# The block order of TensorE, and who rounds the staged expert rows

## The chip, the cores and the metric

One core of a Trainium2 chip runs the whole kernel in one launch. The time is the device time of an execution in microseconds (us). Before the change the median of three runs is 1381.29 us (1379.74 to 1384.87).

## The reference

The input x is 32 sequences of 128 rows and 512 columns, with a context of the same shape. Two gated residual steps follow each other:

```python
x = x + tanh(g_xattn) * attention(layernorm(x), ctx, Wq, bq, Wk, bk, Wv, bv)   # 8 heads of 16, over 512 positions
x = x + tanh(g_ffn) * ffn(layernorm(x), ...)
# attention: q, k, v = projections + bias; softmax(q k / sqrt(16)) v, in each head
# ffn: h = rmsnorm(x) * rms_weight; probs = softmax(h @ router_w); top 2 of 8 experts, weights normalised
#      moe = sum of w_e * (silu(h @ w_gate_e) * (h @ w_up_e)) @ w_down_e, plus one shared expert of the same form
```

In the attention the 128 rows of a sequence are the channels and the 512 columns are the positions. All is float32.

## The kernel before

The kernel is written engine by engine: each engine has its own list of instructions, and semaphores order them across engines. Within an engine the written order is the order of work.

The first stage is a pipeline over the 32 sequences. `TURNS` runs i from -3 to 31. In turn i TensorE works on the scores and values of sequence i, on the row maxima of sequence i + 1, on projections of sequences i + 2 and i + 3, and on the token transposes and router logits of sequence i - 3. A turn has 32 slots s, which TensorE takes in eight blocks of four (`GROUP`). In one block before the change:

1. `exp_scores` (L847) for s and s + 1: two score products in two row halves of the array, each into a bank of its own. With `take_bank` (L788) the three banks of `turning` go round among score products and side products, and a product waits until the last reader of its bank is done. For scores that is ScalarE's exponential (L1342).
2. `max_scores` (L823) twice: four score products of the next sequence into two pairs of banks, whose row maxima VectorE takes (L1080, L1086). A pair of banks is used again two `max_scores` later.
3. `exp_scores` for s + 2 and s + 3.
4. At s = 0 and s = 16 `turn_maxima` (L838, L844), which turns the maxima of half a sequence.
5. `values` (L878, L887) of the block before: it waits for the four exponentials of that block (`s_exp`) and sums over four blocks in one bank, `pv_ps`. The first of each four (s = 4 and s = 20) also waits for `s_u`, until ScalarE's `take_values` (L1358, L1363) has copied the bank.
6. Side products: `turn_tokens` (L865, L862) at s = 12, `router_logits` (L870, L874) at s = 16, `project` (L800, L812 and L818) at s = 8, 24 and 28.

ScalarE walks the same slots one by one. `exponential(i, s)` comes first in each slot, then what belongs to the slot: `take_maxima` at 3 and 19, `take_values` at 4 and 20 (`VALUES_LATE` + 1 = 4), the copy of the turned tokens at 15 (L1370), the evacuation of the projections at 11, 27 and 31, and at s = 13 (`STAGE_AT`) `staged_high`.

Beside this runs the staging of expert weights: the 30 rows of experts 3 to 7 come one per turn from HBM (`load_staged`, L477), are scaled by the RMS weight, split into a rounded part HI and a rest LOW, and stored again (`store_staged`, L483). ScalarE makes HI (L1372 to L1381), GpSimd scales the raw row in place (L700) and makes LOW (L701). GpSimd also normalises (L631, L675), splits the projections (L642) and adds the attention to x (L651).

The second stage, from about 870 us on, is the feed-forward part: 32 jobs of the shared expert and then 71 routed jobs, with L930 as its products. The change touches nothing of it.

Of the kernel before, what the change touches and what calls it, by code (L numbers as in the profile page):

```python
# [21 lines left out]
DMA = 16  # L22
# [3 lines left out]
HI, LOW = range(2)  # L26
# [6 lines left out]
STEPS = HEADS * KT  # L33
# [10 lines left out]
GROUP = 4  # L44
EXPERTS = 8
FF = 256
CHUNKS = L // P
# [5 lines left out]
SLOTS = 4  # L53
IN_PLACE = SLOTS - 1
EARLY = 3
STAGE_AT = 13
LOADED = 2 * W_ROWS * DMA
CHUNK = 16
SPARES = 3
# [22 lines left out]
def build(nc, x_d, ctx_d, g_xattn_d, g_ffn_d, wq_d, bq_d, wk_d, bk_d, wv_d, bv_d, rms_d, router_d, w_d, out_d):  # L82
# [6 lines left out]
    with es:  # L89
        def sem(name):  # L90
            return es.enter_context(nc.semaphore(name))

        def sb(name, shape, dt=F32):
            return es.enter_context(nc.sbuf_tensor(name, shape, dt))
# [37 lines left out]
        staged = [staged_both[:, part, :] for part in range(2)]  # L132
# [59 lines left out]
        staged_raw = w_shared[:, 0, :]  # L192
# [19 lines left out]
        w_rms = sb("w_rms", [P, CHUNKS])  # L212
# [49 lines left out]
        s_const = sem("s_const")  # L262
# [34 lines left out]
        s_raw = sem("s_raw")  # L297
        s_sh = sem("s_sh")
        s_sl = sem("s_sl")
        s_sst = sem("s_sst")  # L300
# [62 lines left out]
        STAGED = [(e, r) for e in range(IN_PLACE, EXPERTS) for r in range(W_ROWS)]  # L363
# [12 lines left out]
        n_const = 5  # L376
# [4 lines left out]
        def is_b(b):  # L381
            return 0 <= b < B
# [227 lines left out]
        def _(pool):  # L610
            links = [0]

            def link(ins):
                links[0] += 1
                ins.then_inc(s_pool, 1)
                pool.wait_ge(s_pool, links[0])
# [25 lines left out]
            def split(b, n):  # L642
                pool.wait_ge(s_evac, 3 * b + n + 1)
                pool.wait_ge(s_part, 2 * b + n)
                pool.wait_ge(s_cp[n], COPIES * DMA * b)
                hi, lo = parts[n]
                nc.gpsimd.tensor_copy(hi, proj[n]).then_inc(s_hi, 1)
                pool.wait_ge(s_hi, 2 * b + n + 1)
                nc.gpsimd.tensor_tensor(lo, proj[n], hi.bitcast(F32), ALU.subtract).then_inc(s_part, 1)
# [41 lines left out]
                nc.gpsimd.tensor_scalar(tok, xs[:, b, :], r, nmr2[:, b:b + 1], ALU.mult, ALU.add).then_inc(s_h, 1)  # L691
                pool.wait_ge(s_h, b + 1)

            def staged_low(k):
                pool.wait_ge(s_sh, k + 1)
                if k:
                    pool.wait_ge(s_sst, DMA * k)
                r = STAGED[k][1]
                if r < CHUNKS:
                    link(nc.gpsimd.tensor_scalar(staged_raw, staged_raw, w_rms[:, r:r + 1], None, ALU.mult))  # L700
                nc.gpsimd.tensor_tensor(staged[LOW], staged_raw, staged[HI].bitcast(F32), ALU.subtract  # L701
                                        ).then_inc(s_sl, 1)

# [15 lines left out]
            for i in TURNS:  # L719
                if is_b(i + 2) and i + 2 > 0:  # L720
                    split(i + 2, 1)
                if is_b(i + 4):
                    normalise(i + 4)
                if is_b(i - 2):
                    tokens(i - 2)
                if 0 <= i + 2 < len(STAGED):
                    staged_low(i + 2)
                for b in range(CHUNK):
                    if i == CHUNK + 6 + b // 2:
                        scatter(b)  # L730
                if is_b(i - 1):
                    add_attention(i - 1)
                if is_b(i + 3) and i + 3 > 0:
                    split(i + 3, 0)
# [49 lines left out]
        def _(pe):  # L784
# [38 lines left out]
            def max_scores(b, u):  # L823
                g, w = divmod(u // 2, GROUP * KT // 2)
                j, qt = divmod(w, KT)
                n = STEPS * b + u
                if u == 0:
                    for kind in range(2):
                        pe.wait_ge(s_cp[kind], COPIES * DMA * (b + 1))
                pair = n // 2  # L830
                if pair >= M_PAIRS:
                    pe.wait_ge(s_mx, pair - M_PAIRS + 1)
                for a in range(2):
                    rows, h = slice(LANE * a, LANE * a + STACK), GROUP // 2 * g + j
                    nc.tensor.matmul(m_ps[pair % M_PAIRS][:, a, :], q_stack[b % 3][rows, h, qt * P:(qt + 1) * P],  # L835
                                     k_stack[b % 3][rows, h, :], start=True, stop=True).then_inc(s_ms, 1)
# [41 lines left out]
            def values(b, r):  # L878
                g, kt = divmod(r, KT)
                pair = 8 * b + r  # L880
                pe.wait_ge(s_exp, STEPS * b + GROUP * (r + 1))
                if r == 0:
                    pe.wait_ge(s_evac, 3 * b + 3)
                if kt == 0 and pair:
                    pe.wait_ge(s_u, pair // KT)
                for j in range(GROUP):
                    last = nc.tensor.matmul(pv_ps[2 * DH * j:2 * DH * (j + 1), :], v_ones[b % 3][:, kt, GROUP * g + j, :],  # L887
                                            probs[pair % 3][:, j, :], start=(kt == 0), stop=(kt == KT - 1))
                last.then_inc(s_pv, 1)
# [75 lines left out]

            for i in TURNS:
                for s in range(0, STEPS, GROUP):
                    if is_b(i):
                        exp_scores(i, s)
                        exp_scores(i, s + 1)  # L970
                    if is_b(i + 1):
                        max_scores(i + 1, s)
                        max_scores(i + 1, s + 2)
                    if is_b(i):
                        exp_scores(i, s + 2)
                        exp_scores(i, s + 3)
                    if s + 3 == MAX_AT[1] and is_b(i):
                        turn_maxima(i, 1)
                    if s + 3 == MAX_AT[0] and is_b(i + 1):
                        turn_maxima(i + 1, 0)  # L980
                    if s == 0 and is_b(i - 1):
                        values(i - 1, STEPS // GROUP - 1)
                    if s and is_b(i):
                        values(i, s // GROUP - 1)
                    if s == TURN_TOKENS_AT and is_b(i - 3):
                        turn_tokens(i - 3)
                    if s == LOGITS_AT and is_b(i - 3):
                        router_logits(i - 3)
                    if s in PROJECT_AT and is_b(i + PROJECT_AT[s][0]):
                        project(i + PROJECT_AT[s][0], PROJECT_AT[s][1])  # L990
                    if s + 3 == COUNT_SLOT and i > CHUNK and (i - 3) % CHUNK == 0:
                        count_choices((i - 3) // CHUNK - 1)
                    if i == B - 1 and s == FIRST_JOB_AT:
                        gate_up(0)
# [332 lines left out]
        def _(act_e):  # L1327
# [41 lines left out]
                    act_e.wait_ge(s_hts, DMA * b)  # L1369
                nc.scalar.copy(tok_t.rearrange("p c n -> p (c n)"), bank_of["tokens", b]).then_inc(s_hf, 1)  # L1370

            def staged_high(k):  # L1372
                act_e.wait_ge(s_raw, DMA * (k + 1))
                if k:
                    act_e.wait_ge(s_sl, k)
                    act_e.wait_ge(s_sst, DMA * k)
                r = STAGED[k][1]
                if r < CHUNKS:
                    nc.scalar.mul(staged[HI], staged_raw, w_rms[:, r:r + 1]).then_inc(s_sh, 1)
                else:  # L1380
                    nc.scalar.copy(staged[HI], staged_raw).then_inc(s_sh, 1)  # L1381

            def exponentials(c):
                act_e.wait_ge(s_ch, c + 1)
                nc.scalar.activation(top[:, 4, :], top[:, 3, :], ACT.Exp).then_inc(s_ex, 1)
# [1 line left out]
            for i in TURNS:  # L1387
                if i == -2:
                    act_e.wait_ge(s_const, n_const * DMA)
                    nc.scalar.activation(tgates[:], gates[:], ACT.Tanh).then_inc(s_tanh, 1)  # L1390
                for s in range(STEPS):
                    if is_b(i):
                        exponential(i, s)
                    if s == MAX_AT[1] and is_b(i):
                        take_maxima(i, 1)
                    if s == MAX_AT[0] and is_b(i + 1):
                        take_maxima(i + 1, 0)
                    if s == EXP_SLOT and i > CHUNK and (i - 3) % CHUNK == 0:
                        exponentials((i - 3) // CHUNK - 1)
                    if s == STAGE_AT and 0 <= i + 2 < len(STAGED):  # L1400
                        staged_high(i + 2)
                    if s == TURN_TOKENS_AT + 3 and is_b(i - 3):
                        take_turned(i - 3)
                    if s == VALUES_LATE + 1 and is_b(i - 1):
                        take_values(i - 1, 1)
                    if s == STEPS // 2 + VALUES_LATE + 1 and is_b(i):
                        take_values(i, 0)
                    if s in EVAC_AT and is_b(i + EVAC_AT[s][0]):
                        evacuate(i + EVAC_AT[s][0], EVAC_AT[s][1])
# [104 lines left out]
```

## Time and profile before

| | |
|---|---|
| median of three runs | 1381.29 us |
| the profiled execution | 1384.91 us |
| its span | 1383.0 us |
| mean granted clock | 0.981 |
| PE busy | 1324.3 us (96%) |
| DVE busy | 891.0 us (64%) |
| ACT busy | 846.3 us (61%) |
| POOL busy | 712.8 us (52%) |

PE is TensorE's matmuls, PEld its weight loads, DVE is VectorE, ACT ScalarE, POOL GpSimd. A row of a timeline merges instructions of one line that follow each other ("x2"); its length goes from the first start to the last end. The end of a matmul is modelled, so the distance between two starts says more than a length. "[0.42 <-ACT arena L1348]" is idle time before the row and the instruction that ended it.

### The profile page before, as it was taken

The numbers are of one execution on the slowest core, as the hardware profiler recorded it, in microseconds if no ns is written. First come the engines' busy times: TensorE is split into PE (matmuls) and PEld (weight loads), VectorE is DVE, ScalarE is ACT, GpSimd is POOL, SyncE is SP. The second block draws the span as 40 slices with busy tenths as digits, with TensorE's granted clock in tenths as the row PEclk, the third lists the DMA queues.
The fourth block names the chain that finished last, engine by engine and source line by source line (L and its number), as shares of the span: only waits on it lengthen the run. The fifth ranks groups of instructions, "written<-read, shape, count | busy, mean of one in ns | idle before, by whom it ended". The sixth has DMA issues, their size and how long they took to land.

```text
span 1383.0 us, 27057 instructions
## 1 busy us (share of the span) xinstructions
PE 1324.3 (96%) x9190; PEld 756.8 (55%) x9190; DVE 891.0 (64%) x1176; ACT 846.3 (61%) x1714; POOL 712.8 (52%) x948
## 2 busy tenths in 40 slices
PE   5999999999999999999999999999799999999997
PEld 2344444444444444344444443677688888888885
DVE  6778787887787788887877777367454333333332
ACT  1588778778788787787787778342334333333332
POOL 7345655555655655557776533103614555555553
PEclk7799999999999999999999999999999999999999
DMA  6546555545555555546756742537855888886665
GB/s 180 150 126 174 174 140 157 172 139 156 170 141 166 158 140 158 152 133 154 177 130 147 143 98 84 185 122 142 101 172 110 212 208 213 176 188 108 109 111 78
DMA packets 123840, 205.83 MB, mean 149 GB/s; under 512 B 28005, under 2 KB 29676, under 8 KB 123710
## 3 DMA queue, kind: packets, MB, share of 16 engines
q1 hardware_dynamic: 105454, 166.74, 44.6%
q0 software_dynamic: 18256, 37.38, 14.8%
q8 instruction: 79, 1.29, 0.4%
q14 instruction: 51, 0.42, 0.1%
HBM read 82.34 MB, written 61.94 MB: 104 GB/s over the span
## 4 chain that ended last, share of the span: by engine, by line
PE 81%; issue 7%; DVE 4%; DMA 3%; POOL 2%; ACT 1%; POOLq 1%; SPq 0%; ACTq 0%
PE m_banks L930 21%; PE bank L857 21%; PE bank L887 18%; PE m_banks L835 9%; PE bank L812 4%; PE bank L862 3%; DVE row_max L1086 2%; PE bank L818 2%; DMA arena<-ht_d 2%; POOL xs L754 1%; PE bank L844 1%; PE bank L874 1%; PE bank L952 1%; DMA out<-xs,arena 1%; POOLq L760 1%
## 5 line engine op out<-in xcount | busy, mean ns | idle before, releaser
L1086 DVE TENSOR_REDUCE row_max<-m_banks 128x2 f32<-128x1024 f32 x512 | 606.3, 1216 | 147.1 <-PE m_banks L835 146.6
L1348 ACT ACTIVATE arena<-bank 128x512 f32<-128x512 f32 x1024 | 540.8, 608 | 77.8 <-PE bank L857 77.4
L857 PE MATMUL bank<-q_stack,k_stack 49*128 49x512 f32 x1024 | 359.7, 484 | 5.3 <-ACT arena L1348 4.1
L857 PEld LDWEIGHTS bank<-q_stack,k_stack 49*128 49x128 f32 x1024 | 143.3, 185 | 282.5 <-ACT arena L1348 203.4
L887 PE MATMUL bank<-arena 128*32 128x512 f32 x2048 | 286.5, 610 | 4.5
L766 POOL DMA_INDIRECT out<-xs,arena x71 | 112.6, 1586 | 158.9 <-ACT xs L1439 122.8
L835 PE MATMUL m_banks<-k_stack,q_stack 48*128 48x512 f32 x1024 | 175.9, 412 | 8.1 <-DVE row_max L1086 7.8
L930 PE MATMUL m_banks<-w_ring,h_hi 128*128 x568 | 183.0, 403 | 0.0
L1428 ACT ACTIVATE arena<-m_banks 128x256 f32<-128x256 f32 x103 | 39.5, 384 | 187.1 <-PE m_banks L930 187.0
L835 PEld LDWEIGHTS m_banks<-k_stack,q_stack 48*128 48x128 f32 x1024 | 101.6, 191 | 40.7 <-DVE row_max L1086 31.8
L930 PE MATMUL m_banks<-w_ring,h_lo 128*128 x284 | 111.7, 393 | 0.0
L930 PEld LDWEIGHTS m_banks<-w_ring,h_hi 128*128 128x128 f32 x568 | 101.4, 189 | 18.4
L1279 DVE TENSOR_TENSOR arena<-arena,m_banks 128x256 f32<-128x256 f32 x71 | 29.9, 421 | 115.8 <-ACT arena L1428 115.8
L709 POOL DMA_INDIRECT map_d<-meta,slots x64 | 64.6, 1010 | 64.8 <-DVE slots L1162 46.4
L656 POOL TENSOR_TENSOR arena<-arena 128x512 f32<-128x512 f32 x32 | 41.2, 1286 | 103.6 <-DMA arena<-rden_d 98.6
L1273 DVE TENSOR_TENSOR act_lo<-bank,act_hi 128x256 fp32r<-128x256 f32 x71 | 30.1, 424 | 96.5 <-ACT act_hi L1445 96.5
L1439 ACT ACTIVATE xs<-m_banks,arena 128x512 f32<-128x512 f32 x71 | 48.8, 687 | 71.0 <-PE m_banks L930 71.0
L1335 ACT ACTIVATE arena<-bank,bias 128x512 f32<-128x512 f32 x64 | 44.0, 688 | 75.9 <-PE bank L812 75.9
L930 PE MATMUL m_banks<-w_ring,act_hi 128*128 x284 | 87.5, 389 | 1.4 <-DVE act_lo L1273 1.4
L754 POOL DMA_INDIRECT xs<-h_d,arena x71 | 69.7, 982 | 33.9 <-issue 21.0
L812 PE MATMUL bank<-arena 128*32 128x512 f32 x512 | 71.7, 634 | 12.5 <-POOL arena L639 7.5
L887 PEld LDWEIGHTS bank<-arena 128*32 128x32 f32 x2048 | 52.2, 108 | 56.6 <-issue 32.7
(176 smaller groups left out, 1779.7 us busy)
## 6 DMA issues: line engine op xcount, KB each, us to landing
k_stack<-arena SPq DMA_DIRECT2D x192, 128.0 KB
q_stack<-arena SPq DMA_DIRECT2D x192, 128.0 KB
split_d<-staged SPq DMA_DIRECT2D x30, 512.0 KB, 5.2
w_ring<-split_d SPq DMA_DIRECT2D x60, 256.0 KB, 4.1
arena<-in_w SPq DMA_DIRECT2D x36, 256.0 KB, 5.6
arena<-in_ctx SPq DMA_DIRECT2D x32, 256.0 KB, 3.7
xs<-in_x SPq DMA_DIRECT2D x32, 256.0 KB, 4.2
arena<-arena SPq DMA_DIRECT2D x64, 128.0 KB, 3.3
```

The source lines that it names most:

```text
L709: nc.gpsimd.indirect_dma_start(map_d, bass.IndirectOffsetOnAxis(ap=slots[:, k, b:b + 1], axis=0), meta[:, k, b, :], None).then_inc(s_sc2, DMA)
L754: nc.gpsimd.indirect_dma_start(gathered[i % IN_RING], None, h_d, bass.IndirectOffsetOnAxis(ap=ids[:, i:i + 1], axis=0)).then_inc(s_got[i % ...
L766: nc.gpsimd.indirect_dma_start(out_d, bass.IndirectOffsetOnAxis(ap=ids[:, i:i + 1], axis=0), y_sb[i % OUT_RING], None, compute_op=ALU.add) ...
L812: last = nc.tensor.matmul(out[c, :], (wk, wq)[n][:, c], ctx_in[b % 2] if n == 0 else xn[b % 2], start=True, stop=True)
L835: nc.tensor.matmul(m_ps[pair % M_PAIRS][:, a, :], q_stack[b % 3][rows, h, qt * P:(qt + 1) * P], k_stack[b % 3][rows, h, :], start=True, st ...
L857: nc.tensor.matmul(out, k_stack[b % 3][rows, h, kt * P:(kt + 1) * P], q_stack[b % 3][rows, h, :], start=True, stop=True).then_inc(s_es, 1)
L887: last = nc.tensor.matmul(pv_ps[2 * DH * j:2 * DH * (j + 1), :], v_ones[b % 3][:, kt, GROUP * g + j, :], probs[pair % 3][:, j, :], start=( ...
L930: last = nc.tensor.matmul(out, v[:, c, :], weights(j, part, first_row + c), start=(c == 0 and n == 0), stop=(c == chunks - 1 and n == 2))
L1086: nc.vector.reduce_max(pair, m_ps[(STEPS * b + u) // 2 % M_PAIRS], AX_X).then_inc(s_mx, 1)
L1335: nc.scalar.activation(proj[n], bank_of["projection", b, n], ACT.Identity, bias=bias[:, n:n + 1]).then_inc(s_evac, 1)
L1348: nc.scalar.activation(probs[group % 3][:, j, :], bank_of["scores", b, s], ACT.Exp, scale=float(DH) ** -0.5).then_inc(s_exp, 1)
L1439: nc.scalar.activation(y_sb[i % OUT_RING], Y_PS[j % 2], ACT.Copy, scale=wts[:, i:i + 1]).then_inc(s_yrt, 1)
```

## The change

In each block TensorE now issues the two `max_scores` first, then `exp_scores` for s and s + 1, then `values` of the block before, then `exp_scores` for s + 2 and s + 3, then `turn_maxima` and the side products. The rounding of the staged rows (HI) moves from ScalarE's slot 13 to GpSimd, into the place where GpSimd made LOW: wait for the load, scale in place, cast to HI, subtract to LOW. Slots of ScalarE, VectorE and SyncE are as before.

```diff
--- before.py
+++ after.py
@@ -53,7 +53,6 @@
 SLOTS = 4
 IN_PLACE = SLOTS - 1
 EARLY = 3
-STAGE_AT = 13
 LOADED = 2 * W_ROWS * DMA
 CHUNK = 16
 SPARES = 3
@@ -691,13 +690,17 @@
                 nc.gpsimd.tensor_scalar(tok, xs[:, b, :], r, nmr2[:, b:b + 1], ALU.mult, ALU.add).then_inc(s_h, 1)
                 pool.wait_ge(s_h, b + 1)
 
-            def staged_low(k):
-                pool.wait_ge(s_sh, k + 1)
+            def split_staged(k):
+                pool.wait_ge(s_raw, DMA * (k + 1))
+                if k == 0:
+                    pool.wait_ge(s_const, n_const * DMA)
                 if k:
                     pool.wait_ge(s_sst, DMA * k)
                 r = STAGED[k][1]
                 if r < CHUNKS:
                     link(nc.gpsimd.tensor_scalar(staged_raw, staged_raw, w_rms[:, r:r + 1], None, ALU.mult))
+                nc.gpsimd.tensor_copy(staged[HI], staged_raw).then_inc(s_sh, 1)
+                pool.wait_ge(s_sh, k + 1)
                 nc.gpsimd.tensor_tensor(staged[LOW], staged_raw, staged[HI].bitcast(F32), ALU.subtract
                                         ).then_inc(s_sl, 1)
 
@@ -724,7 +727,7 @@
                 if is_b(i - 2):
                     tokens(i - 2)
                 if 0 <= i + 2 < len(STAGED):
-                    staged_low(i + 2)
+                    split_staged(i + 2)
                 for b in range(CHUNK):
                     if i == CHUNK + 6 + b // 2:
                         scatter(b)
@@ -965,12 +968,16 @@
 
             for i in TURNS:
                 for s in range(0, STEPS, GROUP):
+                    if is_b(i + 1):
+                        max_scores(i + 1, s)
+                        max_scores(i + 1, s + 2)
                     if is_b(i):
                         exp_scores(i, s)
                         exp_scores(i, s + 1)
-                    if is_b(i + 1):
-                        max_scores(i + 1, s)
-                        max_scores(i + 1, s + 2)
+                    if s == 0 and is_b(i - 1):
+                        values(i - 1, STEPS // GROUP - 1)
+                    if s and is_b(i):
+                        values(i, s // GROUP - 1)
                     if is_b(i):
                         exp_scores(i, s + 2)
                         exp_scores(i, s + 3)
@@ -978,10 +985,6 @@
                         turn_maxima(i, 1)
                     if s + 3 == MAX_AT[0] and is_b(i + 1):
                         turn_maxima(i + 1, 0)
-                    if s == 0 and is_b(i - 1):
-                        values(i - 1, STEPS // GROUP - 1)
-                    if s and is_b(i):
-                        values(i, s // GROUP - 1)
                     if s == TURN_TOKENS_AT and is_b(i - 3):
                         turn_tokens(i - 3)
                     if s == LOGITS_AT and is_b(i - 3):
@@ -1369,17 +1372,6 @@
                     act_e.wait_ge(s_hts, DMA * b)
                 nc.scalar.copy(tok_t.rearrange("p c n -> p (c n)"), bank_of["tokens", b]).then_inc(s_hf, 1)
 
-            def staged_high(k):
-                act_e.wait_ge(s_raw, DMA * (k + 1))
-                if k:
-                    act_e.wait_ge(s_sl, k)
-                    act_e.wait_ge(s_sst, DMA * k)
-                r = STAGED[k][1]
-                if r < CHUNKS:
-                    nc.scalar.mul(staged[HI], staged_raw, w_rms[:, r:r + 1]).then_inc(s_sh, 1)
-                else:
-                    nc.scalar.copy(staged[HI], staged_raw).then_inc(s_sh, 1)
-
             def exponentials(c):
                 act_e.wait_ge(s_ch, c + 1)
                 nc.scalar.activation(top[:, 4, :], top[:, 3, :], ACT.Exp).then_inc(s_ex, 1)
@@ -1397,8 +1389,6 @@
                         take_maxima(i + 1, 0)
                     if s == EXP_SLOT and i > CHUNK and (i - 3) % CHUNK == 0:
                         exponentials((i - 3) // CHUNK - 1)
-                    if s == STAGE_AT and 0 <= i + 2 < len(STAGED):
-                        staged_high(i + 2)
                     if s == TURN_TOKENS_AT + 3 and is_b(i - 3):
                         take_turned(i - 3)
                     if s == VALUES_LATE + 1 and is_b(i - 1):
```

## Rows read from the trace of the kernel before

**Rows 1.** The page's busy time by engine (part 1), its chain (part 4)
```profile
PE 1324.3 (96%) x9190; PEld 756.8 (55%) x9190; DVE 891.0 (64%) x1176; ACT 846.3 (61%) x1714; POOL 712.8 (52%) x948
...
PE 81%; issue 7%; DVE 4%; DMA 3%; POOL 2%; ACT 1%; POOLq 1%; SPq 0%; ACTq 0%
```

**Rows 2.** The page's part 5: group | busy, mean | idle before, releaser
```profile
L1086 DVE TENSOR_REDUCE row_max<-m_banks 128x2 f32<-128x1024 f32 x512 | 606.3, 1216 | 147.1 <-PE m_banks L835 146.6
...
L857 PEld LDWEIGHTS bank<-q_stack,k_stack 49*128 49x128 f32 x1024 | 143.3, 185 | 282.5 <-ACT arena L1348 203.4
```

**Rows 3.** Timeline of TensorE's matmuls, one turn: start us, us, engine, line, operation, count
```profile
483.34 0.50 PE L857 MATMUL bank<-q_stack,k_stack 49*128 49x512 f32 x2
...
485.09 1.06 PE L887 MATMUL bank<-arena 128*32 128x512 f32 x8
486.09 0.50 PE L857 MATMUL bank<-q_stack,k_stack 49*128 49x512 f32 x2
486.43 0.63 PE L835 MATMUL m_banks<-k_stack,q_stack 48*128 48x512 f32 x4
486.90 0.87 PE L857 MATMUL bank<-q_stack,k_stack 49*128 49x512 f32 x2
487.70 1.06 PE L887 MATMUL bank<-arena 128*32 128x512 f32 x8
488.58 1.06 PE L818 MATMUL bank<-arena 128*32 128x128 f32 x32
489.57 0.49 PE L857 MATMUL bank<-q_stack,k_stack 49*128 49x512 f32 x2
...
492.29 0.66 PE L862 MATMUL bank<-ident,arena 128*128 128x128 f32 x4
492.87 0.55 PE L857 MATMUL bank<-q_stack,k_stack 49*128 49x512 f32 x2
...
495.59 0.64 PE L874 MATMUL bank<-w_router,arena 128*32 128x8 f32 x32
496.16 0.50 PE L857 MATMUL bank<-q_stack,k_stack 49*128 49x512 f32 x2
...
509.14 0.50 PE L857 MATMUL bank<-q_stack,k_stack 49*128 49x512 f32 x2
```

**Rows 4.** Timeline of TensorE's weight loads in the same turn
```profile
486.67 0.18 PEld L857 LDWEIGHTS bank<-q_stack,k_stack 49*128 49x128 f32 x1
487.27 0.18 PEld L857 LDWEIGHTS bank<-q_stack,k_stack 49*128 49x128 f32 x1 [0.42 <-ACT arena L1348]
487.70 0.16 PEld L887 LDWEIGHTS bank<-arena 128*32 128x32 f32 x8 [0.24 <-issue]
...
494.11 0.18 PEld L857 LDWEIGHTS bank<-q_stack,k_stack 49*128 49x128 f32 x1 [0.32 <-ACT arena L1348]
494.67 0.13 PEld L844 LDWEIGHTS bank<-ident,row_max 128*16 128x16 f32 x2 [0.37 <-issue]
```

**Rows 5.** Timeline of ScalarE in the same turn
```profile
483.88 0.60 ACT L1348 ACTIVATE arena<-bank 128x512 f32<-128x512 f32 x1 [0.58 <-PE bank L857]
484.37 0.58 ACT L1363 COPY arena<-bank 128x512 f32<-128x512 f32 x1
...
486.62 2.07 ACT L1348 ACTIVATE arena<-bank 128x512 f32<-128x512 f32 x4 [0.19 <-PE bank L857]
...
491.18 0.72 ACT L1379 ACTIVATE staged<-arena,w_rms 128x512 fp32r<-128x512 f32 x1
```

**Rows 6.** Timeline of GpSimd in the same turn
```profile
500.20 1.29 POOL L656 TENSOR_TENSOR arena<-arena 128x512 f32<-128x512 f32 x1 [3.29 <-DMA arena<-rden_d]
...
503.79 0.61 POOL L647 CAST arena<-arena 128x512 fp32r<-128x512 f32 x1
```

**Rows 7.** Timeline of TensorE's matmuls two turns later
```profile
557.14 0.50 PE L857 MATMUL bank<-q_stack,k_stack 49*128 49x512 f32 x1 [1.35 <-ACT arena L1348]
```

**Rows 8.** Busy time in a stretch: window, PE, PEld, DVE, ACT, POOL, clock, DMA
```profile
557.90:561.30 3.40, 3.40 (x15) 0.88 (x18) 2.42 (x3) 1.73 (x4) 1.78 (x2) 0.50 0.25 63
```

## Prediction

> **What bounds the kernel now.** I read the page's shares and its chain first [rows 1]: TensorE is busy for 1324.3 of 1383.0 us and holds 81% of the chain that ended last. ScalarE is busy for 846, VectorE for 891, GpSimd for 713 us, all far below the span. Then the groups by line [rows 2]: VectorE's maxima take 606 us, and the weight loads of the score products L857 (1024 of them, so 32 in each of 32 turns) stood 203 us behind ScalarE's exponentials L1348. So TensorE's own queue sets the time, with a short wait for ScalarE in most blocks. Then the timeline of one turn on TensorE [rows 3]: from the block of s = 4 to the same block a turn later it takes 509.14 - 483.34 = 25.80 us. A turn is eight blocks. I call the first two score products of a block pair A, the last two pair B, and V the value products.
>
> From these rows come the prices, all as start to start. A to the maxima 0.34 (486.09 to 486.43), the two pairs of maxima 0.47 together (486.43 to 486.90), V to a pair of scores 1.00 (485.09 to 486.09), V to a side product 0.88 (487.70 to 488.58), a projection 0.99 (488.58 to 489.57), the token transposes 0.58 (492.29 to 492.87), the router's logits 0.57 (495.59 to 496.16) [rows 3]. The second product of pair B starts 0.60 behind where its first had its weights (486.67 to 487.27), since its bank is that of A's first product, and that one's exponential has to end: L857 waited 0.42 there, of which about 0.37 delay the matmul (the first one started at 486.90). From there to V it is 0.42 [rows 3, 4]. On ScalarE the exponential starts 0.54 behind its product (483.34 to 483.88), the next ones follow every 0.49 ((2.07 - 0.60) / 3), each lasts 0.60, and the matmul that waited starts some 0.05 to 0.08 behind the end [rows 3, 5].
>
> **What the change does to one block.** Work per block stays the same; only the order changes, to maxima, A, V, B, side product. Two dependences that lay loose become tight.
>
> *V against the exponentials.* V needs all four exponentials of the block before. Before, B was issued ahead of V, so a whole block lay between. Now B is issued behind V, and the next V comes after two pairs of maxima and A: by TensorE alone 0.34 + 0.47 + about 0.32 = 1.13 behind B. The exponentials of B end at 0.54 + 0.49 + 0.60 = 1.63, so V starts at 1.71 and the next B 1.00 later: 2.71 for a plain block, against 2.75 before (483.34 to 486.09) [rows 3, 5]. The 0.37 of bank wait goes and 0.58 of wait for exponentials takes its place; what is late next is ScalarE again.
>
> *V against the copy of the values.* At s = 4 and s = 20 V opens a new sum in the one bank pv_ps, which L1363 must have copied, and ScalarE issues that copy behind the exponential of this block's first product (the slot s = VALUES_LATE + 1 is not changed). In the trace: product 483.34, exponential 483.88, copy 484.37 to 484.95, V 485.09, that is 1.75 behind A [rows 3, 5]. Before, B and the maxima lay inside these 1.75 us and V lost some 0.1. Now V stands ahead of B in the queue, and B, the next maxima and everything behind V wait with it. This can't be hidden, since the copy depends on A's exponential by program order alone.
>
> *Side products.* They now stand between B and the maxima. Before they followed V. The price of leaving scores for V is seen in 0.42 from the last score to V where 0.23 would be its columns (half of the 0.47 for two pairs) [rows 3, 4]; a side product now pays that too, 0.42, or 0.58 where its first instruction waits for more than one semaphore, as at L844 (a score at 494.11, L844 at 494.67 and 0.03 more); where I don't know which, I take 0.50 [rows 4].
>
> The Trainium skill, TensorEngine Tiling, section Key Properties, says that a change of tiling mode drains TensorE, and not a change of tile. The trace agrees with 0.42 against 0.23 [rows 4]. Without the drain the six blocks with side products would be about 0.2 shorter each, 1.2 a turn, and the sum below some 37 us smaller.
>
> **A turn, B to B.** Every term in us, from the prices above.
> s 0 to 4 (maxima turned): 0.58, L844 0.30 (one record is 0.1 to 0.3, so this is an estimate between a drained and a running one), maxima to maxima to A 0.34 + 0.24, A at 1.46; its exponential at 2.00, the copy ends 1.07 later, V 0.14 behind that (484.95 to 485.09), at 3.21; + 1.00 = 4.20.
> 4 to 8: 2.71.
> 8 to 12 (projection): 0.50 + 0.99 + 0.34 + 0.24 + 0.32 + 1.00 = 3.39; before 3.48.
> 12 to 16 (tokens): 0.50 + 0.58 + 0.34 + 0.24 + 0.34 + 1.00 = 3.00; before 3.30.
> 16 to 20 (maxima turned, logits): the logits take the bank of B's first product, whose exponential ends at 1.14, so they start at 1.22, not at 0.68; + 0.57 + 0.58, A at 2.37, V 1.75 behind it at 4.12; + 1.00 = 5.12.
> 20 to 24: 2.71. 24 to 28 and 28 to 0 (projections): 3.39 each; before up to 3.65.
> Sum 27.91, against 25.80: 2.1 us more a turn. VectorE needs 2 x 1.22 = 2.43 us of maxima in a block [rows 2], under each of these, so it doesn't bind.
> 27 turns are of this kind: 57 us. The other five lack tokens and logits, or projections, but have both copy waits; at 1.7 us (twice 1.75 + 1.00 + 0.34 + 0.47 = 3.56, less 2.75) they add 8 us. Together 65.
>
> **The rounding of staged rows.** ScalarE loses 30 instructions of 0.72 us (491.18) [rows 5]. It is not the engine in the way at s = 13, where 4 exponentials fill 2.07 of a 3.3 us block; I take 0, at most 0.1 a turn or 3 us gained (it lies ahead of two exponentials). GpSimd gets 30 casts; the same cast of 128x512 takes 0.61 (503.79) [rows 6]. They lie ahead of L656, which stood idle for 3.29 us until the reciprocals landed [rows 6]. I take 0; without that cover it is 30 x 0.61 = 18 us, and the store of the staged rows on SyncE would be late by as much. GpSimd now also waits for the row's load itself, issued a turn earlier.
>
> **The sum.** The profiled run took 1384.9 us (span 1383.0); + 65, less 1 for ScalarE's lighter load, = 1449. The profiled run lies 3.6 above the median of 1381.3, so for the median I predict 1445.
>
> **The rivals.**
> (a) The sides are cheaper than I price them (weights loaded ahead, no bank wait of the logits, 0.3 a side block): only the copy waits remain, some 1.2 a turn: 1381 + 37 = 1418. For it: V to side costs only 0.88. Against: the 0.42 at every score to V.
> (b) The clock falls too. It stood at 0.50 from 557.90 on, that is 1.2 GHz, behind a product that had waited 1.35 us (557.14) [rows 7, 8]. The change makes a 1.2 us wait twice a turn, the second right behind logits of 8 columns. If every second turn has one stretch at 0.50 as long as this one (557.90 to 561.30) and loses 1.4 us in it (an estimate: V's 0.88 and half a projection a second time, since the waits don't grow with the clock), it is 16 x 1.4 = 22 more, up to 45 with one a turn: 1467 to 1490. Against it: the new waits are shorter than that one, and the waits of 0.4 in each block never lowered it.
> (c) Faster. The bank wait of pair B (0.37 in eight blocks, 3.0 a turn) goes and V hardly waits: if the copy at s = 4 and 20 were out before A is issued and the exponentials were done 1.2 us behind B, plain blocks would fall to VectorE's 2.43 and the turn to 24.4: 31 x 1.4 = 43 less, 1338. It decides from the point at which V starts less than 1.5 us behind the block's B. Against it: ScalarE's order puts the copy behind A's exponential, and 1.63 is the sum of three measured durations.
> (d) No change: the gain on bank waits equals the copy waits, 1381. For it: plain blocks come out even.
>
> **How the numbers follow.** Forecast 0.54, (a) 0.16, (b) 0.18, (c) 0.07, (d) 0.05. The forecast's own terms are uncertain by 0.1 in each of some six places of a turn, so 1426 to 1464. The range for 8 in 10 reaches into (a) and (b): 1412 to 1476. Of the outcomes, about 0.5% (7 us) can be told from no change: slower 0.89, within 0.04, faster 0.07.
>
> **What would show it.** In the timeline of a late turn: V at s = 4 and 20 starting 1.75 us behind pair A with B behind it; blocks of 4 to 8 still 2.7 us; a turn of about 27.9 us; the weight loads of L887 waiting for ScalarE (L1348 and L1363) where L857 did; idle of ScalarE waiting for L857 larger. No wait for GpSimd's L701 in the row stores, and L656 still idle for some 2 us. The prediction is wrong if the turn comes out below 25.8, if V at s = 4 starts earlier than 1.5 us behind A, or if more than some 15 stretches show a granted clock of 0.50.

## The result, and the profile after

The changed kernel took 1447.7 us (median of four runs, 1442.4 to 1454.8) against 1381.9 us before: 1.048 times as long, interval 1.043 to 1.053. The prediction was 1445, slower. The profiled run took 1446.75 us, its span is 1444.9, that is 61.9 more than before.

The page of the kernel after: busy time by engine, the chain, and groups of part 5, as in [rows 1, 2]. The exponentials' line is now L1351 (was L1348), the copy of the values L1366 (L1363), scores L860 (L857), V L890 (L887), maxima L838 (L835).

```profile
PE 1319.2 (91%) x9190; PEld 716.7 (50%) x9190; DVE 889.8 (62%) x1176; ACT 853.4 (59%) x1684; POOL 730.8 (51%) x978
...
PE 72%; issue 9%; ACT 8%; DVE 4%; DMA 4%; POOL 2%; POOLq 1%; SPq 0%; ACTq 0%; DVEq 0%
...
L1351 ACT ACTIVATE arena<-bank 128x512 f32<-128x512 f32 x1024 | 557.1, 598 | 227.4 <-PE bank L860 226.5
L890 PE MATMUL bank<-arena 128*32 128x512 f32 x2048 | 284.0, 627 | 70.0 <-ACT arena L1366 68.8
```

TensorE's busy time hardly moved (1324.3 to 1319.2), and its share fell from 96% to 91%: its idle time rose from 58.7 to 125.7 us, which is more than the whole loss. Busy time is not pure work, though: a stretch at half clock makes it longer, as turn 31 shows below. ScalarE entered the chain, 8% for 1%. The value products V now wait 68.8 us for the copy of the values, 63 times 1.1 us. Before, their group stood idle for 4.5 us in all:

```profile
L887 PE MATMUL bank<-arena 128*32 128x512 f32 x2048 | 286.5, 610 | 4.5
```

TensorE's matmuls in one turn of the kernel after, columns as in [rows 3]; in brackets the idle time before and what ended it.

```profile
452.29 0.49 PE L860 MATMUL bank<-q_stack,k_stack 49*128 49x512 f32 x2
452.71 0.39 PE L847 MATMUL bank<-ident,row_max 128*16 128x128 f32 x2
453.03 0.83 PE L838 MATMUL m_banks<-k_stack,q_stack 48*128 48x512 f32 x4
453.70 0.75 PE L860 MATMUL bank<-q_stack,k_stack 49*128 49x512 f32 x2
455.43 1.07 PE L890 MATMUL bank<-arena 128*32 128x512 f32 x8 [0.98 <-ACT arena L1366]
456.43 0.51 PE L860 MATMUL bank<-q_stack,k_stack 49*128 49x512 f32 x2
...
458.10 1.06 PE L890 MATMUL bank<-arena 128*32 128x512 f32 x8
459.10 0.50 PE L860 MATMUL bank<-q_stack,k_stack 49*128 49x512 f32 x2
...
462.44 0.50 PE L860 MATMUL bank<-q_stack,k_stack 49*128 49x512 f32 x2
...
465.53 0.51 PE L860 MATMUL bank<-q_stack,k_stack 49*128 49x512 f32 x2
465.96 0.39 PE L847 MATMUL bank<-ident,row_max 128*16 128x128 f32 x2
466.72 0.44 PE L877 MATMUL bank<-w_router,arena 128*32 128x8 f32 x32 [0.36 <-ACT arena L1351]
467.08 0.73 PE L838 MATMUL m_banks<-k_stack,q_stack 48*128 48x512 f32 x4
467.65 0.40 PE L860 MATMUL bank<-q_stack,k_stack 49*128 49x512 f32 x2
469.30 1.06 PE L890 MATMUL bank<-arena 128*32 128x512 f32 x8 [1.25 <-ACT arena L1366]
470.30 0.50 PE L860 MATMUL bank<-q_stack,k_stack 49*128 49x512 f32 x2
...
479.61 0.49 PE L860 MATMUL bank<-q_stack,k_stack 49*128 49x512 f32 x2
```

Read it from pair B to pair B, as the prediction did. 452.29 to 456.43 is the block 0 to 4, 4.14 us; 456.43 to 459.10 the plain block 4 to 8, 2.67; to 462.44 the projection, 3.34; to 465.53 the tokens, 3.09; to 470.30 the block 16 to 20, 4.77; the last three take 9.31. Together 27.32 us, against 25.80 before [rows 3]: 1.5 more.

ScalarE over the first copy wait, the same columns:

```profile
454.21 0.60 ACT L1351 ACTIVATE arena<-bank 128x512 f32<-128x512 f32 x1
454.71 0.58 ACT L1366 COPY arena<-bank 128x512 f32<-128x512 f32 x1
...
456.96 1.58 ACT L1351 ACTIVATE arena<-bank 128x512 f32<-128x512 f32 x3 [1.17 <-PE bank L860]
```

The chain is all there: product 453.70, its exponential 454.21, the copy 454.71 to 455.29, V at 455.43; then ScalarE does the second exponential of pair A and sits idle for 1.17 us, because pair B stands behind V. The stall is handed from one engine to the other.

TensorE's weight loads in the plain block that follows:

```profile
457.61 0.18 PEld L860 LDWEIGHTS bank<-q_stack,k_stack 49*128 49x128 f32 x1 [0.42 <-ACT arena L1351]
458.10 0.16 PEld L890 LDWEIGHTS bank<-arena 128*32 128x32 f32 x8 [0.31 <-ACT arena L1351]
```

The bank wait of 0.42, which stood at pair B's second product before [rows 4], has not gone. It moved to pair A's second product, which now takes the bank of B's first.

**Where 62 us went.** Stretches of whole turns, and the clock in them (busy time by engine, granted clock, DMA share, GB/s), columns as in [rows 8]. After:

```profile
532.90:677.60 144.70, 130.19 (x1084) 49.55 (x1082) 114.76 (x137) 104.57 (x202) 79.11 (x122) 0.95 0.49 139
867.00:895.40 28.40, 25.80 (x166) 9.80 (x164) 20.49 (x22) 18.50 (x37) 5.80 (x10) 0.82 0.18 60
895.40:928.20 32.80, 29.31 (x136) 10.28 (x134) 8.23 (x17) 17.68 (x34) 5.85 (x10) 0.64 0.13 42
902.00:926.00 24.00, 22.31 (x103) 7.47 (x102) 5.67 (x11) 12.69 (x24) 4.07 (x4) 0.50 0.18 57
```

Before, the same turns (18 to 22, 30, and 31 up to the stage behind it):

```profile
506.00:640.00 134.00, 126.90 (x1088) 54.38 (x1084) 113.20 (x137) 103.90 (x206) 74.56 (x116) 0.99 0.53 148
821.90:844.60 22.70, 22.39 (x172) 9.23 (x168) 19.85 (x21) 18.41 (x38) 5.83 (x10) 1.00 0.22 73
844.60:867.30 22.70, 19.96 (x138) 8.08 (x134) 11.73 (x19) 16.24 (x33) 5.96 (x10) 1.00 0.19 60
```

The 26 turns from 3 to 28 cost 1.51 more each: 39 us. Turns 18 to 22 took 10.7 more instead of 5 x 1.5: 3 us beyond that, at a clock of 0.95 for 0.99. Turn 30 grew by 5.7 and turn 31 by 10.1, where the order explains some 1.6 each; in turn 31 the clock stood at 0.50, that is 1.2 GHz, for 24 us on end. Turn 29 came out 1.6 shorter than before, where a half-speed stretch lay in it (27.15 us; 23.9 in the kernel of experiment 2, where none did). The first turns and both ends make the rest. In all some 49 us are the order itself, turn by turn (39 for the 26 turns and about 1.6 for each of the other six), and the remaining 13 us or so come with the clock and the uneven turns. This split is an estimate. Over the whole run the mean clock went from 0.981 to 0.968.

The staging left one trace on GpSimd (timeline of a turn, as [rows 6]):

```profile
464.53 0.61 POOL L702 CAST staged<-arena 128x512 fp32r<-128x512 f32 x1
...
469.47 1.28 POOL L655 TENSOR_TENSOR arena<-arena 128x512 f32<-128x512 f32 x1 [2.97 <-DMA arena<-rden_d]
```

GpSimd is busy for 18.0 us more, 30 casts of 0.61, and still stands idle 2.97 us for the reciprocals.

### The profile page after: what moved, and what is told of

It reads as the page before. It is cut to its first block, busy times and chain, and to the rows that moved or that the text cites. A ratio compares the mean times of both kernels' runs of the same rounds, so it can differ in the third digit from the quotient of the medians.

```text
span 1444.9 us, 27029 instructions
## 1 busy us (share of the span) xinstructions
PE 1319.2 (91%) x9190; PEld 716.7 (50%) x9190; DVE 889.8 (62%) x1176; ACT 853.4 (59%) x1684; POOL 730.8 (51%) x978
## 4 chain that ended last, share of the span: by engine, by line
PE 72%; issue 9%; ACT 8%; DVE 4%; DMA 4%; POOL 2%; POOLq 1%; SPq 0%; ACTq 0%; DVEq 0%
PE m_banks L933 20%; PE bank L890 18%; PE bank L860 14%; PE m_banks L838 9%; ACT arena L1351 4%; PE bank L815 4%; PE bank L865 3%; DVE row_max L1089 2%; DMA arena<-ht_d 2%; PE bank L821 2%; ACT arena L1366 2%; POOL xs L757 1%; PE bank L955 1%; PE bank L877 1%; DMA out<-xs,arena 1%
## 5 line engine op out<-in xcount | busy, mean ns | idle before, releaser
L1351 ACT ACTIVATE arena<-bank 128x512 f32<-128x512 f32 x1024 | 557.1, 598 | 227.4 <-PE bank L860 226.5
L890 PE MATMUL bank<-arena 128*32 128x512 f32 x2048 | 284.0, 627 | 70.0 <-ACT arena L1366 68.8
L860 PE MATMUL bank<-q_stack,k_stack 49*128 49x512 f32 x1024 | 285.4, 472 | 2.2 <-ACT arena L1351 2.0
L860 PEld LDWEIGHTS bank<-q_stack,k_stack 49*128 49x128 f32 x1024 | 123.4, 189 | 277.9 <-issue 162.5
L838 PE MATMUL m_banks<-k_stack,q_stack 48*128 48x512 f32 x1024 | 195.9, 456 | 7.3 <-DVE row_max L1089 7.2
L838 PEld LDWEIGHTS m_banks<-k_stack,q_stack 48*128 48x128 f32 x1024 | 90.2, 191 | 98.5 <-issue 68.0
L890 PEld LDWEIGHTS bank<-arena 128*32 128x32 f32 x2048 | 42.6, 109 | 156.2 <-ACT arena L1351 114.3
L678 POOL TENSOR_SCALAR arg<-mv 128x1 f32<-128x1 f32 x32 | 6.2, 192 | 166.1 <-DVE mv L1061 166.1
L646 POOL CAST arena<-arena 128x512 fp32r<-128x512 f32 x62 | 37.8, 609 | 97.3 <-ACT arena L1338 96.4
```

The source lines that it names most:

```text
L860: nc.tensor.matmul(out, k_stack[b % 3][rows, h, kt * P:(kt + 1) * P], q_stack[b % 3][rows, h, :], start=True, stop=True).then_inc(s_es, 1)
L1351: nc.scalar.activation(probs[group % 3][:, j, :], bank_of["scores", b, s], ACT.Exp, scale=float(DH) ** -0.5).then_inc(s_exp, 1)
```

## Experiments

"Block" and "turn" are as above, pair B to pair B unless it says otherwise. Line numbers are those of each kernel.

**1. The order alone: ScalarE rounds the staged rows again.**

```
-                nc.gpsimd.tensor_copy(staged[HI], staged_raw).then_inc(s_sh, 1)
...
+                    if s == STAGE_AT and 0 <= i + 2 < len(STAGED):
+                        staged_high(i + 2)
```

> Only TensorE's new block order; ScalarE still rounds the staged rows at s = 13. Theory 1 (the order makes V wait, staging is free): about the time of the changed kernel, 1448 us, at most 3 us more since ScalarE keeps 30 x 0.72 us; a turn of 27.3 us with the block 12 to 16 up to 0.1 longer. Rival (the cast on GpSimd delays something): 15 to 18 us less than the changed kernel, near 1430.

Measured 1453.1 us (1450.3 to 1456.8), 1.050 times before, interval 1.046 to 1.054. Its undisturbed turns take 27.3 to 27.5 us. The order is the whole loss. The time is 5.4 above that of the changed kernel, where at most 3 were expected; the two intervals against before overlap, and its turns 3 to 28 hold five stretches at half speed, for two in the changed kernel.

**2. The staging alone: TensorE's order as before.**

```
-                    if is_b(i + 1):
-                        max_scores(i + 1, s)
-                        max_scores(i + 1, s + 2)
                     if is_b(i):
                         exp_scores(i, s)
                         exp_scores(i, s + 1)
+                    if is_b(i + 1):
+                        max_scores(i + 1, s)
+                        max_scores(i + 1, s + 2)
...
+                    if s and is_b(i):
+                        values(i, s // GROUP - 1)
```

> Only the rounding of the staged rows moves to GpSimd; TensorE's order is that of before. Theory 1: 1379 to 1382 us, a turn of 25.8 us or up to 0.1 less. Rival (GpSimd is late): 1395 to 1400 us, with waits of SyncE's row stores or of the additions of the attention.

Measured 1383.7 us, ratio 1.000, interval 0.997 to 1.002, with a turn of 25.79 for 25.80. GpSimd's slack covers the casts; ScalarE's 0.72 us a turn was worth nothing here and 0.1 to 0.2 a turn in the new order (27.31 against up to 27.5 in experiment 1).

**3. The changed kernel with the copy one block earlier: behind pair A's exponentials and ahead of pair B's, instead of behind the first exponential of the next block.** The values of the half turn before are complete by then, so the copy can go into slots 1 and 17.

```
-                    if s == VALUES_LATE + 1 and is_b(i - 1):
+                    if s == 1 and is_b(i - 1):
                         take_values(i - 1, 1)
-                    if s == STEPS // 2 + VALUES_LATE + 1 and is_b(i):
+                    if s == STEPS // 2 + 1 and is_b(i):
                         take_values(i, 0)
```

> The changed kernel with ScalarE's copy of the values at slots 1 and 17 instead of 4 and 20, so it no longer stands behind the exponential of the block's pair A. Theory 1 (copy wait): the blocks 0 to 4 and 16 to 20 fall from 4.14 and 4.76 to about 2.7 and 3.4, bound by the four exponentials; the turn from 27.3 to 24.6, and with it the half-clock stretches go: 1350 to 1365 us, under the kernel before. Rival 1 (the price lies in leaving and entering the tiling of the side products): the two blocks lose at most 0.5 each and the time stays above 1415. Rival 2 (the clock is most of it): the number of stretches at 0.50 stays and so do 20 us of the loss.

Measured 1374.4 us (1369.6 to 1381.6), 0.993 times before, interval 0.991 to 0.996. So it is 73 us faster than the changed kernel and slightly faster than the one before, but outside the range that I gave. TensorE in the block 0 to 4:

```profile
447.15 0.50 PE L860 MATMUL bank<-q_stack,k_stack 49*128 49x512 f32 x2
...
448.57 0.84 PE L860 MATMUL bank<-q_stack,k_stack 49*128 49x512 f32 x2
449.34 1.06 PE L890 MATMUL bank<-arena 128*32 128x512 f32 x8
450.34 0.50 PE L860 MATMUL bank<-q_stack,k_stack 49*128 49x512 f32 x2
```

The block is 3.19 us (447.15 to 450.34) for 4.14, V is 0.77 behind A for 1.73, without a wait for the copy. The turn is 25.2, where 24.6 was expected: block 0 to 4 takes 3.19, not 2.7, and block 16 to 20 takes 3.54, not 3.4. In the first, pair A's second product waits for its bank (0.84 us for the two, where 0.40 to 0.50 is usual). The rest of the miss is in turns 18 to 21, by the stretches of whole turns of this kernel:

```profile
496.20:609.00 112.80, 104.56 (x870) 38.30 (x868) 93.79 (x116) 83.85 (x162) 59.42 (x94) 0.94 0.51 143
145.00:495.00 350.00, 338.76 (x3006) 128.07 (x3008) 285.95 (x307) 289.11 (x556) 210.77 (x331) 1.00 0.56 160
```

At 25.2 a turn these four should take 101 us and take 113, with the clock at 0.94. In the regular turns the gain is 26 x 0.6 = 16 us on the kernel before; 7 of them go back here, since the same four turns exceed their pace by 5 us in the kernel before.

**4. The same copy slots in the order of the kernel before.** Edit: that of experiment 3, in the kernel before.

> The kernel before with the same earlier copy. Theory 1: there the copy wait lay under pair B, only some 0.1 us showed in each of two blocks of a turn, so 1372 to 1382 us. Rival (the early copy helps whatever the order, by freeing ScalarE): 20 us or more faster, under 1362.

Measured 1536.1 us (1526.1 to 1556.2), 1.115 times before, interval 1.107 to 1.124. A plain miss of mine. ScalarE, then TensorE:

```profile
459.51 0.59 ACT L1363 COPY arena<-bank 128x512 f32<-128x512 f32 x1 [1.45 <-PE bank L887]
460.00 1.09 ACT L1348 ACTIVATE arena<-bank 128x512 f32<-128x512 f32 x2
```

```profile
457.14 0.98 PE L857 MATMUL bank<-q_stack,k_stack 49*128 49x512 f32 x2
...
460.65 0.99 PE L857 MATMUL bank<-q_stack,k_stack 49*128 49x512 f32 x2 [1.21 <-ACT arena L1348]
```

Before, V of s = 0 stands behind pair B. A copy in slot 1 waits for that V, and B's exponentials stand behind the copy on ScalarE; pair A of the next block then waits 1.21 us for a bank. The early slot pays only with V ahead of B: order and slot have to be chosen together. These waits are not the whole price. The few turns without a stretch at half speed take 28.5 us, 2.7 more than before, which would be some 70 us over 26 turns; the loss is 152. From 160 to 930 us the clock was 0.92:

```profile
160.00:930.00 770.00, 697.96 (x5466) 289.89 (x5466) 531.29 (x579) 528.87 (x1035) 385.79 (x586) 0.92 0.49 130
```

**5. The changed kernel with the copy one exponential later (slots 5 and 21).**

```
-                    if s == VALUES_LATE + 1 and is_b(i - 1):
+                    if s == VALUES_LATE + 2 and is_b(i - 1):
```

> The changed kernel with the copy of the values one slot later, 5 and 21, so behind both exponentials of pair A. Theory 1 (V waits for that copy and everything behind V with it): one exponential pitch of 0.49 more in the blocks 0 to 4 and 16 to 20, 4.63 and 5.25, a turn of 28.3: 1448 + 31 = 1479, and up to 20 us above that if the longer waits bring more stretches at half clock. Rival (the copy isn't what V waits for): within 3 us of 1448.

Measured 1544.6 us (1539.9 to 1547.6), 1.114 times before, interval 1.110 to 1.118. One undisturbed turn and its V:

```profile
135.07 0.75 PE L860 MATMUL bank<-q_stack,k_stack 49*128 49x512 f32 x2
137.29 1.07 PE L890 MATMUL bank<-arena 128*32 128x512 f32 x8 [1.47 <-ACT arena L1366]
```

V is 2.22 behind A, 0.49 later than in the changed kernel: one exponential, as the chain says. The turn is 28.30, exactly what was expected. But the time is a miss: 1479 to 1499 was expected. Of turns 3 to 28 this is the only one without a stretch at half speed; the next takes 33.6 us. That turn, and the stretch up to 990 us:

```profile
132.30:160.60 28.30, 24.73 (x218) 9.54 (x216) 20.68 (x22) 20.80 (x41) 14.03 (x23) 1.00 0.49 142
160.00:990.00 830.00, 733.58 (x5748) 282.87 (x5744) 561.93 (x610) 559.11 (x1070) 417.15 (x636) 0.88 0.47 125
```

A mean clock of 0.88 means a quarter of these 830 us at half speed. 1 us more of wait in a turn costs about 30 us by the chain and took 97. The other two thirds lie in turns with stretches at half speed.

**6. Side products moved.** Three kernels: tokens, logits and projections between V and pair B (6a); every side product between A and V (6b); 6b with the copy of experiment 3 (6c). The edit of 6a:

```
                     if s and is_b(i):
                         values(i, s // GROUP - 1)
+                    if s == TURN_TOKENS_AT and is_b(i - 3):
+                        turn_tokens(i - 3)
+                    if s == LOGITS_AT and is_b(i - 3):
+                        router_logits(i - 3)
+                    if s in PROJECT_AT and is_b(i + PROJECT_AT[s][0]):
+                        project(i + PROJECT_AT[s][0], PROJECT_AT[s][1])
                     if is_b(i):
                         exp_scores(i, s + 2)
```

> The changed kernel with token transposes, logits and projections between V and pair B, so that they follow V in its tiling and one switch of tiling out of four goes in those blocks. Theory 1 (a block lasts from pair B to the V that waits for its exponentials, 1.7, and on to the next B): the projection's 1.87 from V to B adds to 1.7, 3.58 against 3.32, but the logits come off the wait; turn 27.1 to 27.7, time 1438 to 1460. Rival (the switches of tiling are the price): 0.3 less in each of five blocks, a turn of 25.8, 1400.

> The changed kernel with all side products (logits ahead of the turned maxima) between pair A and V: one switch of tiling less, and the side product runs while V would wait for the exponentials of B. The copy stays at slots 4 and 20. Theory 1: projections 3.02 instead of 3.32, tokens 2.75, the blocks into s = 0 and 16 2.7 to 2.8, the two blocks with the copy 3.56: a turn of 24.3 to 24.8, so 1350 to 1370. Rival (VectorE's 21.2 us of work a turn and its order bind first): a turn above 25, 1375 or more.

> Both: side products between pair A and V, and the copy at slots 1 and 17. Theory 1: the two copy blocks fall to 2.7 too; TensorE alone would need 22.7 a turn, VectorE at 21.2 is nearly full, so 23.0 to 23.8: 1305 to 1335. Rival (VectorE binds, and the router's choices in turns 18 to 21 cost more): 24.5 a turn and 10 us more there, 1350 to 1360.

Measured 1661.3 us (1.204 times before, 1.195 to 1.212), 1800.9 (1.296, 1.291 to 1.301) and 1614.6 (1.166, 1.160 to 1.173). All three are misses. Only 6b's rival leaves room for its number (1375 or more), but it blames VectorE, while TensorE waits for ScalarE there as in the other two. TensorE in 6a, behind a projection, then ScalarE:

```profile
510.17 0.50 PE L860 MATMUL bank<-q_stack,k_stack 49*128 49x512 f32 x2
...
512.42 0.50 PE L860 MATMUL bank<-q_stack,k_stack 49*128 49x512 f32 x2 [1.28 <-ACT arena L1338]
```

```profile
510.70 1.08 ACT L1351 ACTIVATE arena<-bank 128x512 f32<-128x512 f32 x2 [3.11 <-PE bank L860]
511.67 0.69 ACT L1338 ACTIVATE arena<-bank,bias 128x512 f32<-128x512 f32 x1
```

Banks go round in the order in which TensorE asks for them. With a projection ahead of pair B, pair A is the next to need its bank, and ScalarE empties that one (L1338) only behind B's two exponentials. A waits 1.28 us for it. The place of a side product is thus tied to the slot of its reader. In all, TensorE waited 148 us in 6a for the readers of side products (L1338, L1342, L1373) and 62 us for the copy, by the trace's sums of waits; in the changed kernel the copy took 69 and these readers next to nothing. The mean granted clock was 0.900 in 6a and 0.915 in 6c, so here too the waits are only part of the loss.

**7. 6c with the readers two slots earlier.**

```
-EVAC_AT = {27: (3, 0), 31: (3, 1), 11: (2, 2)}
+EVAC_AT = {25: (3, 0), 29: (3, 1), 9: (2, 2)}
...
-                    if s == MAX_AT[1] and is_b(i):
+                    if s == MAX_AT[1] - 2 and is_b(i):
                         take_maxima(i, 1)
...
-                    if s == TURN_TOKENS_AT + 3 and is_b(i - 3):
+                    if s == TURN_TOKENS_AT + 1 and is_b(i - 3):
                         take_turned(i - 3)
```

> Side products between pair A and V, the copy at slots 1 and 17, and the readers of the side products' banks (evacuations, turned tokens, turned maxima) also two slots earlier, behind A's exponentials, so that the next block's A, which takes the side product's bank, doesn't wait until B's exponentials are through. Theory 2, formed from the last four runs (the bank of a side product comes round after two score products, and the order of its reader decides): projections 3.0, tokens 2.8, plain 2.7, a turn of 23 to 24, no stretches at half clock beyond a few, 1315 to 1345 us. Rival (the price of these orders is the switch of tiling or the order of the products as such): blocks with projections stay at 4.5 and the time above 1500.

This and experiment 8 ran in two later sessions, where the kernel before took 1429.9 and 1431.0 us, so only ratios and turns compare with the others. Measured 1429.9 us, ratio 1.000, interval 0.997 to 1.002. The loss of 6c (1.166) is gone, which shows that the slots of the readers were its cause. The gain that I expected did not come: the regular turn is 25.7 us, not 23 to 24. The block with a projection is 3.5 us, not 3.0; TensorE's weight loads:

```profile
456.70 0.18 PEld L860 LDWEIGHTS bank<-q_stack,k_stack 49*128 49x128 f32 x1 [0.42 <-ACT arena L1351]
```

The side product cannot fill this bank wait, since A's second product waits ahead of it in the queue.

**8. The copy one exponential earlier than in the changed kernel (slots 3 and 19)**, the mirror of experiment 5, and again with experiment 3 beside it.

```
-                    if s == VALUES_LATE + 1 and is_b(i - 1):
+                    if s == VALUES_LATE and is_b(i - 1):
```

> The changed kernel with the copy of the values one slot earlier, 3 and 19: it moves past a single exponential, that of pair A. Theory 1 (what costs is that the copy stands behind A's exponential, so that V can start only 1.75 behind A): the copy then follows B's exponentials and ends some 2.35 behind B, V at 2.45, so the block 0 to 4 takes 3.4 to 3.5 instead of 4.14 and 16 to 20 about 3.5 instead of 4.76; a turn of 25.3 to 25.6, 1375 to 1390 us. Rival (it is ScalarE's load, so one slot is worth one exponential): 0.49 less in each, a turn of 26.3, 1410 to 1420.

> The same kernel as copy_one_slot, since on that chip the kernel before took 1430 us too, with waits of 5 us in four late turns that no other run has. Regular turns of 25.6 us. Theory 1: without those waits 1376 to 1386 us, ratio to before 0.995 to 1.002. Rival (the order has a fault of its own in the late turns): 1415 us or more beside a kernel before at 1384.

> The same kernel as copy_early, once more, since it is the fastest so far. Theory 1: a turn of 25.2 us, 3 to 12 us in all lost again in the turns 18 to 21, where VectorE makes the router's choices; ratio to before 0.990 to 0.997. Rival (the gain was that chip's): ratio 1.000 or above.

Measured 1431.6 us beside 1429.9 for the kernel before (ratio 1.000, 0.997 to 1.003), and 1426.8 beside 1431.0 (0.998, 0.996 to 1.000) for the one slot; 1410.0 beside the same 1431.0 (0.985, 0.983 to 0.988) for experiment 3's kernel. The absolute times expected were missed, since these sessions were slower for the kernel before as well; the ratios of the one slot came as expected, that of experiment 3's kernel came out lower than its 0.990 to 0.997. The one slot's TensorE, then ScalarE's copy:

```profile
455.65 0.75 PE L860 MATMUL bank<-q_stack,k_stack 49*128 49x512 f32 x2
456.90 1.07 PE L890 MATMUL bank<-arena 128*32 128x512 f32 x8 [0.50 <-ACT arena L1366]
```

```profile
456.17 0.59 ACT L1366 COPY arena<-bank 128x512 f32<-128x512 f32 x1
```

V is 1.25 behind A and waits 0.50 for the copy, between 0 (experiment 3) and 0.98. Its turn is 25.59 us, within the 25.3 to 25.6 expected, 1.7 below the changed kernel's. So the slot of one copy, moved by one exponential, takes back the whole loss in the regular turns and a little more. That is more than two exponentials (2 x 0.49): in block 0 to 4 it gives back 0.5 us (4.14 to 3.65), in block 16 to 20 it gives back 1.3 (4.77 to 3.45). There the logits hold up pair A, and a copy that comes ahead of A's first exponential no longer waits for A. With slots 1, 3, 4 and 5 the undisturbed turns are 25.2, 25.6, 27.3 and 28.3 us.

Experiment 3's kernel is the fastest of all those run: 0.985 and 0.993 times the kernel before in two sessions.

## Why the prediction was right

It was right in direction, in size (2.7 us below the median) and in what causes it. Two of its terms were off, the price of a regular turn (too high) and the clock (left out), and their errors nearly cancel.

*V against the copy.* Right: 1.73 and 1.65 us behind A, for 1.75 predicted. Experiments 5 and 8 move only the copy by one exponential each way, and V at s = 4 follows it (2.22 and 1.25 behind A); with the copy a block earlier (experiment 3) the wait is gone.

*V against the exponentials.* The size was right, 2.67 for a plain block where 2.71 was predicted. The account of it was half right: the bank wait of 0.42 did not go, it moved to A's second product, and V's weights wait 0.31 behind it, where the prediction had no bank wait and 0.58 for V.

*Side products.* Projections right (3.34 and 3.32 for 3.39), tokens nearly (3.09 for 3.00). From pair B to the turned maxima, where the longer price of 0.58 was put, it took 0.42 and 0.43 us (452.29 to 452.71, 465.53 to 465.96), so the shorter one.

*Block 16 to 20.* Mis-sized: 4.77 for 5.12. The logits started 1.19 behind B as predicted (1.22), but then took 0.36 us to the maxima (466.72 to 467.08), not the 0.57 read before, where V stood ahead of them and a score behind; which of the two neighbours makes the difference, no run shows. V's 1.65 for 1.75 gives the rest.

*The turn.* 27.32 for 27.91. There are 26 regular turns, not 27, and they cost 1.51 us more each, not 2.1: 39 us, where the sum had 57. This is the term of the sum that was wrong.

*The clock.* The sum held nothing for it, and rival (b) put 22 to 45 us on it. Some 13 us go with it and with the uneven turns, in nine stretches at 0.50 ahead of the end for six before, and mostly in turns 30 and 31, which the prediction had priced only by their copy waits. So the rival was partly true at once with the forecast. That the total came out at 1447.7 owes something to luck: with the right turn and nothing for the clock the same sum would have given about 1431 (1381.9 + 49).

*The staging.* Right: nothing, with the cover named (L655 still idle for 2.97 us).

*The rivals.* (a) named a mechanism that was partly at work (cheaper logits), but the 0.42 remained. (c) failed where the prediction said, at the copy's place behind A's exponential; experiment 3 takes that away and lands at 0.993, so even with it (c)'s 1338 is out of reach: its blocks of 2.43 never came, a plain block of a regular turn was 2.67 there too.

**Still open.** What exactly makes the clock fall. The length of the waits does not settle it. Waits of 0.98 and 1.25 us in a turn brought two stretches in turns 3 to 28 of the changed kernel and five in experiment 1; waits of 1.47 and 1.74 us brought them in all but one turn (experiment 5). But in experiment 4 two waits of 1.2 us (1.21 and 1.22), no longer than those of the changed kernel, brought them in 21 of these 26 turns. In the sessions at 1430 us, turns 26 to 29 have stalls that the others don't show, of 3 to 6 us, on VectorE and ScalarE at once (experiment 8, VectorE):

```profile
738.56 0.17 DVE L1074 COPY arena<-bank 128x8 f32<-128x8 f32 x1 [6.32 <-remote]
```

The second stage has some too, the longest 21.5 us on ScalarE in experiment 3's kernel, which from turn 31 on took 20 us more than in its first session. The kernel before was not traced there, so whether such stalls explain its 1430 us isn't shown, nor why experiment 3 gains more there.

## What to carry to other kernels

When two groups swap places in an engine's queue, look past the engine's own times: write down for each group what it waits for and what now stands behind it, and move the other engine's slot (here a copy of 0.58 us) together with it; one slot was worth 1.7 us a turn. Banks given out in rotation tie the order of products to the order of their readers in the same way. When a stall on TensorE returns every turn, allow for more than its own length, and read the granted clock: in experiments 4 and 5 the longer undisturbed turn explains 70 of 152 us and 30 of 97.

## What the runs showed of the hardware

The clock moved more than I had expected: between the changed kernel and experiment 5 the undisturbed turn differs by 1.0 us, and the mean granted clock went from 0.968 to 0.906; in experiment 4, with a turn of 28.5 us and waits of 1.2 us, it was 0.932. From the start of 32 matmuls of 8 columns to the maxima behind them it took 0.36 us. A change of order left TensorE's busy time as it was to 0.4% and cost 4.8% of time.
